# Filler products in front of fifteen jobs of the tensor engine in a two-layer decoder kernel

## What is computed

```
x = x + attention(norm(x))            # attn0: 16 heads of 8, softmax over the keys
x = x + cross_attention(norm(x), ctx) # cross0: 8 heads of 64
x = x + classed_attention(norm(x))    # mixer: 16 heads of 8; tokens split in two classes by a
                                      # similarity scaled between its minimum and maximum (> 0.9)
x = x + delta_rule(norm(x))           # a recurrence over tokens, gated, with a norm of its own
x = x + cross_attention(norm(x), ctx) # cross1: 16 heads of 64
x = x + ffn(norm(x))                  # 128 -> 512, gelu, norm, 512 -> 128; ternary weights
```

## Time and profile before

| | us |
|---|---|
| median of 3 runs | 492.67 |
| lowest, highest | 491.37, 494.96 |
| the profiled execution's own time | 495.16 |
| its span, first to last instruction | 493.3 |

### The profile page before, as it was taken

How to read it: one execution, slowest core, us unless ns; L and a number is a source line. 1 busy time by engine, 2 the same in 40 slices (tenths; PEclk the granted TensorE clock), 3 DMA queues, 4 the chain that set the end, 5 groups by cost and what they waited for, 6 DMA issues and landing times.

```text
span 493.3 us, 7123 instructions
## 1 busy us (share of the span) xinstructions
PE 372.2 (75%) x2667; PEld 206.9 (42%) x2667; DVE 278.2 (56%) x579; ACT 213.7 (43%) x360; POOL 124.0 (25%) x118
## 2 busy tenths in 40 slices
PE   2787698889798687978858465579789796789635
PEld 1543334445555133335435224335345373356514
DVE  3755645675574444554455832779875838572242
ACT  2364564455364223545634322336456433745030
POOL 5000000465350000000011600146766333446100
PEclk9998999999999756889987855769999998989655
DMA  8500000100000000001000000000000000000000
GB/s 219 133 2 1 2 1 1 44 1 0 1 3 0 1 0 0 2 1 34 12 1 0 0 1 0 1 0 1 2 1 1 0 2 1 0 1 12 2 0 11
DMA packets 9655, 6.14 MB, mean 12 GB/s; under 512 B 3723, under 2 KB 8726, under 8 KB 9622
## 3 DMA queue, kind: packets, MB, share of 16 engines
q1 hardware_dynamic: 9622, 5.69, 4.4%
HBM read 5.39 MB, written 0.26 MB: 11 GB/s over the span
## 4 chain that ended last, share of the span: by engine, by line
PE 58%; DVE 24%; ACT 8%; issue 8%; POOL 1%; DMA 0%; SPq 0%; DVEq 0%; POOLq 0%
PE ACC L667 7%; PE PS L632 6%; PE PS L583 5%; PE PS L756 5%; PE PS L765 4%; DVE mx L1195 3%; PE PS L800 3%; DVE mxw L1198 3%; PE PS L623 3%; PE PS L653 2%; PE PS L604 2%; PE PS L773 2%; PE PS L611 2%; PE PS L639 2%; PE ACC L697 2%
## 5 line engine op out<-in xcount | busy, mean ns | idle before, releaser
L1198 DVE TENSOR_REDUCE mxw<-PS 128x2 f32<-128x1024 f32 x48 | 58.5, 1221 | 28.6 <-PE PS L611 28.3
L975 ACT ACTIVATE Pc<-PS 128x1024 f32<-128x1024 f32 x48 | 49.1, 1022 | 24.4 <-PE PS L639 23.3
L529 POOL TENSOR_TENSOR Psum<-Pc 128x512 f32<-128x512 f32 x24 | 31.0, 1293 | 108.7 <-ACT Pc L975 108.0
L1195 DVE TENSOR_REDUCE mx<-PS 128x4 f32<-128x1024 f32 x32 | 38.8, 1223 | 34.2 <-PE PS L604 34.2
L667 PE MATMUL ACC<-Pc,V 128*64 128x256 f32 x384 | 52.9, 397 | 0.0
L531 POOL TENSOR_TENSOR Psum<-Psum,Pc 128x512 f32<-128x512 f32 x24 | 30.4, 1268 | 43.8 <-ACT Pc L975 43.5
L975 ACT ACTIVATE Ps<-PS 128x1024 f32<-128x1024 f32 x32 | 32.7, 1022 | 12.0 <-PE PS L623 10.8
L543 POOL TENSOR_TENSOR mid<-mid 128x256 f32<-128x256 f32 x2 | 1.4, 722 | 132.8 <-ACT mid L1078 132.8
L667 PEld LDWEIGHTS ACC<-Pc,V 128*64 128x64 f32 x384 | 23.7, 138 | 24.2 <-issue 16.0
L532 POOL TENSOR_TENSOR Psum<-Psum,Pc 128x512 f32<-128x512 f32 x24 | 30.7, 1278 | 1.9
L632 PE MATMUL PS<-Qhl,Khl_a 64*128 64x256 f16 x384 | 27.8, 279 | 2.0 <-ACT Pc L975 1.0
(11 more groups left out here) (271 smaller groups left out, 747.0 us busy)
## 6 DMA issues: line engine op xcount, KB each, us to landing
Qm<-mrow SPq DMA_DIRECT2D x64, 0.5 KB, 1.7
wq_c<-in_c_Wq_dram SPq DMA_DIRECT2D x1, 512.0 KB, 5.4
spread<-in_c_Wo_dram SPq DMA_DIRECT2D x1, 512.0 KB
Pc<-in_ctx_dram SPq DMA_DIRECT2D x1, 384.0 KB, 4.3
wk_c<-in_c_Wk_dram SPq DMA_DIRECT2D x1, 384.0 KB, 6.4
wv_c<-in_c_Wv_dram SPq DMA_DIRECT2D x1, 384.0 KB, 7.3
csth<-in_const_dram SPq DMA_DIRECT2D x1, 320.0 KB, 4.9
x<-in_x_dram SPq DMA_DIRECT2D x2, 128.0 KB, 2.3
```

Of the source, the lines that this page charges most:

```text
L529: alone(v.tensor_tensor(t, p[:, :, 0, :], p[:, :, 1, :], ALU.add), "sums_done")
L975: e = A(to, src.rearrange("p a c -> p (a c)"), ACT.Exp, scale=PHASES[name].scale)
L1195: last = v.tensor_reduce(to, src.rearrange("p e (t s) -> p e t s", t=2), AX, ALU.max)
L1198: last = v.tensor_reduce(to, src, AX, ALU.max)
```

## The change

In front of fifteen PE jobs, before the wait for their input, PE now takes the job's bank and writes into it a number of products of constants, `ones_h` with `ones_h` spread to 512 columns, in float16. The job's own products start a new sum there and overwrite them. The first of them all waits for `ones_set` to reach 3, which POOL signals at the start of the kernel. `WARM` gives the number of products for each job.

```diff
+WARM = {
+    job("prep", "mixer", 0, 0): 14,
+    job("turn", "mixer", 0, 0): 4, job("turn", "mixer", 0, 1): 4, job("turn", "mixer", 0, 2): 4,
+    job("rt", "mixer", 0): 6, job("dt", "", 0): 16, job("xt", "", 1, 3): 18, job("yT", "", 0): 12, job("xt", "", 0, 4): 12,
+    job("dt", "", 1): 12, job("sp", "", 1, 1): 5,
+    job("out", "cross1", 1): 6, job("xt", "", 1, 5): 8, job("fT", "", 1): 14, job("ff2", "", 1): 6,
+}
...
+            def keep_busy(j):
+
+                if not warm_ready:
+                    pe.wait_ge(sem("ones_set"), 3)
+                    warm_ready.append(True)
+                dst = take(j)
+                for _ in range(WARM[j]):
+                    mm(dst[:, 0, :], ones_h[:], ones_h[:].unsqueeze(1).to_broadcast([P, 4, P]), start=True, stop=True)
+
+            warm_ready = []
             for j in plan:
                 kind, name, b, u, i = j
+                if j in WARM:
+                    keep_busy(j)
                 if kind == "M":
                     maxima(j)
```

## The result

The changed kernel takes 472.68 us (median of 4, 467.49 to 475.30) beside 493.81 (median of 4, 491.37 to 495.40) for the kernel before: 21.1 us less by the medians, with a ratio of 0.954, 95% interval 0.944 to 0.964. The medians here are of all runs, while every ratio is that of the means of the fast runs alone, without, for one, the slow 475.30 of the changed kernel; by these means the gain is 22.7 us. A repeat in a later group of runs gave 469.24 (6 runs) beside 495.50, ratio 0.949 (0.944 to 0.953), 26.3 us by the medians. The forecast was 468.2, a gain of 24.5, and both times lie in its range. The profiled execution is the slowest of its four, 475.30 with a span of 473.4; the four runs had granted clocks of 0.977, 0.970, 0.960 and 0.959 at 467.5, 471.1, 474.2 and 475.3 us, in order.

What follows compares the result with a forecast made beforehand. PE's work at 1.2 GHz after waits for DVE, often on the path, was taken as the bound. Gains of 30.7 less 6.2 that won't come give 24.5, so 492.67 becomes 468.2 us, range 461.5 to 479.5.

Steps and rivals of the forecast that it cites:

- mixer start and the piece at 197: PE's half-clock work at the mixer's start (9.0) and in the piece at 197.0 (0.8) speeds up: 9.8 us gained.
- rt: The 3.4 us at 217.5, with PE busy throughout, become 1.8 at full clock: 1.6 us gained.
- dt, sp, K: dt of batch 0 (1.0), the first sp (0.8) and the K behind it (1.3 reaching DVE): 3.1 us gained.
- xt 3 to dt of batch 1: From xt 3 to dp, K twice on the chain (1.9 each), dp and its transposition (1.7): 5.5 us gained.
- dt of batch 1 to sp 1,3: Only DVE's idle time, about 3.7, shows as gain, less 1.1 for the uncovered filler: 2.6 us.
- end: out, bias rows, xt, ff1, fT and ff2 in the serial end run at full clock: 8.1 us gained.
- The sum of 30.7: All gains from mixer start to end if the clock then stays up: 30.7 us together.
- all holds: Rival: the clock stays up over every leftover wait, full gain of 30.7 us, 462.0 us; chance 0.20.
- The one uncovered filler: At sp 1,1 five products stand wholly behind the bank's wait: 1.1 us added, 2.1 at half clock.
- What won't come, 6.2: Fillers leave nine waits, prep to fT, partly unfilled; the clock may fall there, so 6.2 us comes off the gain.
- The slow rival: Constant products don't hold the clock, fillers at 0.43 us each outlast their waits: 11.5 us added, 504.2 us; chance 0.04.
- DVE takes over: Rival: the mixer's DVE maxima set the pace, 9.8 becomes 5, delta pieces give half of 11.2: 479; chance 0.07.

Runs made afterwards that it cites:

- all waits filled: Changed kernel with longer fillers, nine products in free bank 5 replacing the five at sp 1,1, and fillers at three more waits: 462.85 us, ratio 0.938.
- the last kernel: Kernel with all waits filled, its nine bank 5 products replaced by the change's five behind the bank's wait at sp 1,1: 465.70 us, ratio 0.943.

## Why the prediction was right

Its steps, against the kernel with all waits filled, are the sizes of the terms:

| term | predicted, clock up | all filled | changed, first profile |
|---|---|---|---|
| mixer start and the piece at 197 | 9.8 | 9.6 | 5.8 |
| rt | 1.6 | 1.1 | 1.1 |
| dt, sp, K | 3.1 | 3.1 | 3.1 |
| xt 3 to dt of batch 1 | 5.5 | 5.7 | 2.9 |
| dt of batch 1 to sp 1,3 | 2.6 | 3.7 | 0.7 |
| end | 8.1 | 8.0 | 7.3 |

- *The sum of 30.7.* The rival "all holds" was put at 462.0, and a kernel in which it holds took 462.85. But the gains are what compares. Between the two profiled spans it is 32.5 us, 31.2 of it in the stages of the table and the other 1.3 in cross1. My sum without the 1.1 of the uncovered filler, which that kernel doesn't have, is 31.8. It has more fillers than the change, so this is no proof for the change itself, but the stages are the same.
- *The one uncovered filler.* Predicted as 1.1 us behind the bank's wait, 2.1 at half clock: 1.07 in the last kernel, 2.1 in the changed one. The stage without it was put at 3.7 and gained 3.7, though only with nine products in the free bank as well; with the wait left empty (14.5 us from sp 1,1 to sp 1,3) the clock fell there.
- *What won't come, 6.2.* The measured gains, 21.1 and 26.3 us, stand around the forecast of 24.5. Right was that the clock falls where a wait is only partly filled, and at fewer than half of the nine leftovers that I had listed: at four in the first profile (prep, xt 3, xt 4, xt 5), at three in the repeat (dt, xt 3, xt 5). The size 6.2 is partly luck. Against the same sum of 30.7 the stages of the first profile lost 9.8 and those of the repeat 4.6. In the first the mixer lost 4.0 where I took 2.0 off, with the first V at half clock (3.38 us), one of the signs of being wrong that I had named, and the last preps and M's ahead of turn 2 too; sp 1,1 lost 1.9 where I took nothing beyond the 1.1; dt and its sp lost nothing where I took 1.1. That fillers lift the clock again is not shown: at xt 3 it fell at 273.9 and was back at 277.4, and the next fillers start at 277.63. The row that I read as the clock surviving 2.13 us (turn 0,5 of cross1) was a lucky one, for it fell there in eight of twelve profiles.
- *The slow rival.* That it can go so is shown by one-row products, 500.4 for my 504.2. Its gauge was too large. I had every filler at 0.43 us, but ahead of dt, sixteen took 4.19 us, 0.26 each, since the clock had not yet fallen, and 0.53 of the wait was left where I took 2.0 of delay; ahead of xt 3, 2.19 were left where I took 1.4 of delay.
- *DVE takes over.* It did not: with the clock up DVE's maxima and PE alternate, and first prep to turn 2 came to 19.4 us in the repeat, from 28.4.
- *Gaps.* On the rule of the Trainium skill (TensorE: Matmul & The Clock Gate, "Why this matters for your kernels") only long idle gaps bring the clock down. The rests of 2.18 us at xt 3 here were followed by falls in all seven profiles, and three kernels with that rest filled had none there.

Open stays what the single longer filler is worth at each place, since those kernels change all at once, and why the clock fell at 168 once behind nineteen products.

## What to carry to other kernels

Where a profile shows PE waiting for another engine and then working at 1.2 GHz on the path, the wait can be filled with products that use the whole array, into the bank of the job behind it, and the gain is that work's time at half clock less its time at full, as far as no other engine holds it. Read each wait's releaser first: in front of a wait for data a filler that ends sooner is free, behind a wait for the very bank it writes it is pure delay and wants another bank. Fill to just under the wait at full clock, for two rests of 1.4 and 1.0 us in a row lost the clock every time here. A filler at half clock lasts twice as long and can itself be waited for.

## What the runs showed of the hardware that I had not expected

- Full occupation of PE isn't enough: busy for 37.60 of 37.60 us, partly with one-row products, it stayed at half clock, and 141 one-row products held nothing where 141 products over 128 rows held it through most waits (500.4 us against 469 to 473).
- Nor are 128 rows always enough to lift it. In the kernel before, PE was busy for all of the first 8.9 us of out, nearly all of it float32 products over 128 rows, and the clock stayed at half; why is open.

```profile
461.10:470.00 8.90, 8.90 (x36) 7.97 (x36) 0.00 (x0) 0.00 (x0) 0.00 (x0) 0.50 0.01 2
```

- Float32 transpositions hold the clock as well as products, 470.2 us with 282 of them.
- Four runs of one kernel differ by 8 us, with mean granted clocks of 0.977 to 0.959. With all waits filled four of six runs lie within 0.7 us of each other.
